# A graph network in two layers: one tile in four chunks of the second layer built by TensorE, its weight matmuls split in 64-row pairs, and the one-hots beside the early chunks made by ScalarE

## The reference

```
h  = max(layernorm(x), 0)
x += relu((segment_sum((h * norm_src)[src], dst) * norm_dst) @ weight + bias)        # layer 0
h  = max(layernorm(x), 0)
w  = (relu(edge_attr_32 @ W1 + b1) @ W2 + b2).reshape(e, 4, 8, 8)                    # per edge
m0 = ALPHA * (einsum(s[src] * sh0, w_000) + C110 * einsum(v[src], sh1, w_110))
m1 = ALPHA * (einsum(s[src], sh1, w_011) + einsum(v[src] * sh0, w_101))
x += segment_sum([m0, m1], dst) + SI_SCALE * (h through si_w0, si_w1)                # layer 1
```

## Time and profile before

| | |
|---|---|
| median of three runs | 4124.31 us |
| the profiled execution | 4122.98 us |
| its span (first to last instruction) | 4121.1 us |
| busy: PE, DVE, ACT, POOL | 3132.6, 2649.4, 1693.6, 3087.7 us |
| layer 0: early chunks gathered / beside early / alone | to 294 / 294 to 873 / 873 to 1978 us |
| layer 1: first to last gather | 1998.8 to 4092.6 us |
| granted TensorE clock, mean | 0.875 |

### The profile page before, as it was taken

One profiled execution on the slowest core, in us unless ns is written; L12 is line 12 of the kernel. 1 busy time (PEld: TensorE's weight loads), 2 busy tenths in 40 slices (PEclk: granted clock), 3 DMA queues, 4 the chain that ended last, 5 costly groups with the idle time before them and its releaser, 6 DMA issues.

```text
span 4121.1 us, 82454 instructions
## 1 busy us (share of the span) xinstructions
PE 3132.6 (76%) x20394; PEld 2298.3 (56%) x20395; DVE 2649.4 (64%) x5843; ACT 1693.6 (41%) x5935; POOL 3087.7 (75%) x3210
## 2 busy tenths in 40 slices
PE   5654444468777777777788888888888888888887
PEld 4544444444444443343466667666677667666676
DVE  8995444455555554454577777777777777777776
ACT  3210000013333333333655555555555555555554
POOL 7767777777777777777677777777777777777775
PEclk9996555568888888988899999999999999999999
DMA  2021111111111111111111111111111111111111
GB/s 56 14 54 39 38 38 38 38 27 23 22 23 23 22 23 22 21 22 21 26 30 28 28 28 29 30 28 28 29 30 29 28 28 29 30 28 28 29 30 18
DMA packets 244961, 119.57 MB, mean 29 GB/s; under 512 B 148880, under 2 KB 226065, under 8 KB 244817
## 3 DMA queue, kind: packets, MB, share of 16 engines
q0 software_dynamic: 102528, 52.70, 9.1%
q1 hardware_dynamic: 131625, 48.99, 5.1%
q10 hardware_dynamic: 10768, 17.44, 1.3%
HBM read 113.94 MB, written 4.92 MB: 29 GB/s over the span
## 4 chain that ended last, share of the span: by engine, by line
POOL 59%; issue 24%; DVE 8%; PE 3%; DMA 1%; DVEq 1%; ACT 1%; POOLq 1%; ACTq 0%; SPq 0%
POOL g L447 59%; DVE acc_b L952 4%; DMA g<-table,idx 1%; PE ps L704 1%; PE ps L738 1%; PE ps L772 1%; ACT onehot L579 1%; DVEq L952 0%; ACT onehot L586 0%; DVE hn L1212 0%; DVE prod_a L1066 0%; DVE ef L1195 0%; ACT root L557 0%; DVE stat L905 0%; DVE stat L902 0%
## 5 line engine op out<-in xcount | busy, mean ns | idle before, releaser
L447 POOL DMA_INDIRECT g<-table,idx x2980 | 2872.1, 964 | 935.1 <-issue 902.5
L828 PE MATMUL ps<-w_s,hid 128*128 128x256 f32 x3328 | 884.8, 417 | 270.0 <-ACT hid L627 220.8
L828 PEld LDWEIGHTS ps<-w_s,hid 128*128 128x128 f32 x3328 | 660.4, 207 | 437.5 <-DVE prod_a L1270 231.3
L579 ACT ACTIVATE onehot<-iota_all,dst_rel 128x68 f32<-128x68 f32 x2648 | 673.8, 337 | 384.4 <-DVEq L1132 319.8
L639 ACT ACTIVATE q<-g,sh 128x32 f32<-128x32 f32 x1664 | 375.4, 308 | 861.5 <-DMA g<-table,idx 861.5
L738 PE MATMUL ps<-split_s,prod_a 128*128 128x512 bf16 x1736 | 572.7, 415 | 34.4 <-DVE prod_a L1057 33.5
L1275 DVE TENSOR_REDUCE msg_b<-prod_b 128x128 f32<-128x1024 f32 x416 | 502.1, 1207 | 0.0
L704 PE MATMUL ps<-onehot,g 128*33 128x68 f32 x2880 | 269.4, 263 | 273.8 <-issue 173.8
L1245 DVE TENSOR_TENSOR vsh<-g,sh 128x192 f32<-128x192 f32 x208 | 81.7, 393 | 580.1 <-ACT q L642 580.1
L704 PEld LDWEIGHTS ps<-onehot,prod_a 128*128 128x128 f32 x3328 | 388.8, 192 | 86.1 <-issue 86.0
L704 PEld LDWEIGHTS ps<-onehot,g 128*33 128x33 f32 x2880 | 233.4, 137 | 344.1 <-issue 327.5
(11 more groups left out here) (132 smaller groups left out, 3437.3 us busy)
## 6 DMA issues: line engine op xcount, KB each, us to landing
g<-table,idx POOLq DMA_INDIRECT x2980
ef<-edge_t SPq DMA_DIRECT2D x208, 128.0 KB
ef<-src_rows ACTq DMA_DIRECT2D x27, 512.0 KB, 3.6
prod_a<-src_rows SPq DMA_DIRECT2D x124, 64.0 KB, 3.0
idx<-src_chunks SPq DMA_DIRECT2D x416, 4.0 KB
g<-x_rows,idx POOLq DMA_INDIRECT x224
sh<-sh_chunks SPq DMA_DIRECT2D x208, 16.0 KB
table<-hn ACTq DMA_DIRECT2D x5, 320.0 KB, 3.5
```

What stands on the lines that cost most here:

```text
L447: pool.indirect_dma_start(out=g[:, j, t, 0:FEAT], out_offset=None, in_=table, in_offset=bass.IndirectOffsetOnAxis(ap=idx[:, j, t:t + 1], a ...
L579: ins = act.activation(onehot[:, b, t, :], iota_all[:, 0:WIN], ACT.Square, scale=-1.0, bias=dst_rel[:, bass.ds(c * TILES + t, 1)])
L828: mm = pe.matmul(w_ps[h][:, t, :], hid[:, h, P * t:P * t + P], w2_s[:, :], start=True, stop=True)
```

## The change

1. In layer 1, from the third iteration on (`ROWS_FROM = 2`, so 50 iterations), the eighth tile of the fourth chunk (`ROWS_AT = 3`) is no longer gathered. It is built as in layer 0: VectorE splits table2 into three bfloat16 parts during the first seven chunks (`split_group`), makes the 7 selection matrices at the end of the fourth chunk (`make_source2`), TensorE runs the 21 matmuls behind the window sums of the first chunk (`source_rows2`), VectorE picks the rows at the end of the second (`choose2`). SyncE loads the groups of table2 and the source numbers, in its queue between the loads that were there.
2. The 256 weights: the hidden values of the two halves of a chunk now lie in partitions 0 to 63 and 64 to 127 of `hid`, `w2_s` stands there twice, and the eight matmuls are four pairs of 64 rows. The bias no longer fits in as a row, so four bfloat16 matmuls of 32 rows by 512 columns write it first, from a tile of ones and b2 in three parts; VectorE prepares that after layer 0. Both halves are asked for in one piece: TensorE waits until both relus are done and both halves of the weights before have been used. The two halves of the hidden layer go to different partitions of one PSUM bank, where they had a bank each; the other bank takes the built rows.
3. In `beside_early` the one-hots come from ScalarE, as in `alone`, and ScalarE's loads of early sources stand between them.
4. The last step of a block writes x in place of xc.

```diff
+    def rows_made_in(i):
+        return not isinstance(i, int) or i >= ROWS_FROM
...
-                    for t in range(tiles):
+                    for t in range(MADE if rows_made and j == ROWS_AT else tiles):
                         pool.indirect_dma_start(
...
+            def onehots_beside(i):
+                for pos in range(len(UNITS)):
...
+                    wait(act, joined1, n)
+                    distances(2 * i + nxt_k if nxt_early else RING * nxt_i + (EARLY + nxt_k),
+                              1 - pos % 2).then_inc(squares1_made, 1)
+                    act.wait_ge(squares1_made, n + 1)
+                    ones_at_zero(1 - pos % 2).then_inc(onehot1_ready, 1)
+                    if nxt_early and not (isinstance(i, int) and 2 * i + nxt_k == EARLY - 1):
+                        next_sources(2 * i + nxt_k)
...
-                        mm = pe.matmul(ps[0:HID, H_BANK + h, at:at + 256], w1_s[row:row + 32, :],
+                        mm = pe.matmul(ps[HID * h:HID * h + HID, H_BANK, at:at + 256], w1_s[row:row + 32, :],
                                        ef[row:row + 32, 512 * (j // 2) + at:512 * (j // 2) + at + 256], start=True,
-                                       stop=True, tile_position=(row, 0))
+                                       stop=True, tile_position=(row, HID * h))
...
-                k = 2 * (RING * i + j) + h
-                pe.wait_ge(hidden_ready, k + 1)
-                wait(pe, weights_used, k - 1)
+                k = 2 * (RING * i + j)
+                pe.wait_ge(hidden_ready, k + 2)
+                wait(pe, weights_used, k)
+                for u in range(4):
+                    h, t = u % 2, u // 2 * 2
+                    rows = slice(32 * u, 32 * u + 32)
+                    pe.matmul(w_ps[h][:, t:t + 2, :], ones_b[rows, :], bias_b[rows, :, :], start=True, stop=False,
+                              tile_position=(32 * u, 0), skip_group_check=True)
                 for t in range(4):
-                    mm = pe.matmul(w_ps[h][:, t, :], hid[:, h, P * t:P * t + P], w2_s[:, :], start=True, stop=True)
-                mm.then_inc(weights_ready, 1)
+                    for h in range(2):
+                        rows = slice(HID * h, HID * h + HID)
+                        mm = pe.matmul(w_ps[h][:, t, :], hid[rows, 0, P * t:P * t + P], w2_s[rows, :], start=False,
+                                       stop=True, tile_position=(HID * h, 0), skip_group_check=True)
...
+            def source_rows2(m):
+                pe.wait_ge(split2_done, GROUPS)
+                pe.wait_ge(source2_ready, m + 1)
+                for k in range(GROUPS):
+                    for n in range(3):
+                        mm = pe.matmul(rows2_ps, source2[:, k, :], split[n][:, k, :],
+                                       start=(k == 0 and n == 0), stop=(k == GROUPS - 1 and n == 2))
...
                     window_sums(c, messages_of(b), j, b, seg2_done, 1)
+                    if j == 0 and rows_made_in(i):
+                        source_rows2(i - ROWS_FROM)
...
+                    if isinstance(c, int) and c < GROUPS:
+                        split_group(c)
+                    if j == ROWS_AT - 2 and rows_made_in(i):
+                        choose2(i - ROWS_FROM, RING * i + ROWS_AT)
+                    if j == ROWS_AT and not (isinstance(i, int) and not ROWS_FROM - 1 <= i < ITERS - 1):
+                        make_source2(i - (ROWS_FROM - 1))
```

More of the change, by code:

```diff
@@ L262, in over_iterations, with over_layer2 @@
             body(ITERS - 1)
+        def over_layer2(eng, body):
+            for i in range(ROWS_FROM):
+                body(i)
+            with eng.Fori(ROWS_FROM, ITERS - 1) as i:
+                body(i)
+            body(ITERS - 1)
+        def rows_made_in(i):
+            return not isinstance(i, int) or i >= ROWS_FROM
         def final_blocks(eng, c):
@@ L437, in _, with gather @@
                       allow_small_or_imprecise_dtypes=True).then_inc(iota_done, 1)
-            def gather(i, table, iteration, free, tiles=TILES):
+            def gather(i, table, iteration, free, tiles=TILES, rows_made=False):
                 for j in range(RING):
@@ L483, in _ @@
             pool.wait_ge(table2_out, 16 * BLOCKS)
-            over_iterations(pool, lambda i: gather(
-                i, table2, i + ITERS, lambda c, j: wait(pool, d_ready, c - RING + 1)))
+            over_layer2(pool, lambda i: gather(
+                i, table2, i + ITERS, lambda c, j: wait(pool, d_ready, c - RING + 1),
+                rows_made=rows_made_in(i)))
         @block.scalar
@@ L838, in layer2 @@
                     b = j % 2
[L839 to L840 removed]
+                    weights(i + (j + 1) // RING, (j + 1) % RING)
                     hidden(i + (j + 2) // RING, (j + 2) % RING)
@@ L1235, in _ @@
             link(dve.tensor_scalar(w2_s[:, 64:256], w2_s[:, 64:256], float(ALPHA), None, ALU.mult))
+            dve.wait_ge(bias_in, 16)
+            link(dve.memset(ones_b, 1.0))
+            link(dve.tensor_scalar(bias_f[:, 0:64], bias_f[:, 0:64], float(ALPHA * C110), None, ALU.mult))
+            link(dve.tensor_scalar(bias_f[:, 64:256], bias_f[:, 64:256], float(ALPHA), None, ALU.mult))
+            for k in range(3):
+                link(dve.tensor_copy(bias_part, bias_f))
+                if k < 2:
+                    link(dve.tensor_tensor(bias_f, bias_f, bias_part, ALU.subtract))
+                for u in range(2):
+                    if k == 0:
+                        link(dve.tensor_scalar(bias_b[:, u, :], bias_part, masks[:, 0:1], None, ALU.mult))
+                    else:
+                        link(dve.scalar_tensor_tensor(out=bias_b[:, u, :], in0=bias_part, scalar=masks[:, k:k + 1],
+                                                      in1=bias_b[:, u, :], op0=ALU.mult, op1=ALU.add))
@@ L1236, in _, with split_group @@
             dve.tensor_scalar(sel_b_s[64:96, :], sel_b_s[64:96, :], float(SI_SCALE), None,
                               ALU.mult).then_inc(weights_scaled, 1)
+            def split_group(k):
+                n = group_rows(k)
+                full = stage2[k % 2][0:n, :]
+                high, middle, rest = (part_s[0:n, k, :] for part_s in split)
+                dve.wait_ge(whole2_in[k % 2], 16 * (k // 2 + 1))
+                link(dve.tensor_copy(high, full))
+                link(dve.tensor_tensor(full, full, high, ALU.subtract))
+                link(dve.tensor_copy(middle, full))
+                dve.tensor_tensor(rest, full, middle, ALU.subtract).then_inc(split2_done, 1)
@@ new lines, in make_source2 @@
+            def make_source2(m):
+                dve.wait_ge(keys2_in, 16 * (m + 1))
+                dve.tensor_scalar(key2, keys2, GROUP_LOG, None, ALU.logical_shift_right).then_inc(key2_ready, 1)
+                dve.wait_ge(key2_ready, m + 1)
+                for k in range(0, GROUPS, 2):
+                    n = min(2, GROUPS - k)
+                    ins = dve.tensor_tensor(source2[:, k:k + n, :], key2[:, None, :].to_broadcast([P, n, P]),
+                                            first[:, k:k + n, None].to_broadcast([P, n, P]), ALU.is_equal)
+                ins.then_inc(source2_ready, 1)
```

165 lines of the change are left out of this document (113 added, 52 removed).

## The result

The changed kernel takes 4222.4 us (median of 4, 4207.5 to 4236.4) where the kernel before took 4124.4: the ratio is 1.0236, with an interval of 1.021 to 1.0261. I had predicted 4057 us and given slower a chance of 0.13. The profiled execution took 4210.9 us, span 4209.1, which is 87.9 more than the profiled execution before.

A forecast was written before the change was run, and what follows sets the result against it. It took GpSimd's gather line, 59% of the chain of waits, as the bound: 4122.98 - 62.9 (gathers) - 12 (one-hots) + 5 (VectorE in layer 1) + 1 (rest) + 3 (even race) = 4057.1 us, range 4037 to 4122.

The forecast's parts named there:

- 50 x 1.259: GpSimd in layer 1: 50 iterations lose one gather of 1.259 us each, 62.9 us saved.
- the condition beside it: A removed gather pays only while TensorE, VectorE and ScalarE can use a chunk faster than GpSimd fetches it.
- part 2: Layer 1's consumers: whether they can follow GpSimd's shortened iteration of 39.0 us; 38.3 forecast, a cover of 0.7 us.
- x = 2.45: Length of TensorE's one-piece weights group per chunk with bias, paired matmuls overlapping: 2.45 us, between 2.2 and 4.6.
- the 38.3: Consumers' iteration in us: four rounds 30.0, built tile 3.6 late, selection matrices and choice 3.9, output 0.8.
- these steps keep their length: Behind the last gather: the 28 us there were to stay as they were.
- Rival A: VectorE's wait for weights: pairs don't overlap or bias is slow; slower, 4341 us at its point; chance 0.13.
- rival B: TensorE: x 2.6 to 3.0, hidden layer unpaired or lower clock; 4060 to 4125 us; chance 0.27.
- One-hots, -12: Early stretch: VectorE one-hots hold up gathers, so moving them to ScalarE saves 12 us.
- rival C: Early stretch: one-hots on VectorE cost gathers nothing, so 4069 us; chance 0.10.
- +5 for VectorE's work in layer 1: The 50 built tiles' VectorE work holds up gathers in layer 1, 0.10 us each: 5 us added.
- +1 for the rest: Splitting table2, preparing the bias and SyncE's new loads: 1 us added, from 0 to +6.

The follow-up runs named there:

- e2: The changed kernel with weights made as before the change, 128-row, unpaired, each half asked for by itself; built tiles stay: 4061.5 us, ratio 0.9847.
- h1: The changed kernel with ten unread matmuls ahead of TensorE's wait before the weights of chunks 1 and 3: 4107.2 us, ratio 0.996.
- e3: The changed kernel with pairs laid over two tiles of the same half, so each half is asked for alone: 4098.7 us, ratio 0.9949.
- h5: e3 with seven unread matmuls in chunk 1 ahead of the second half's weights: 4070.9 us, ratio 0.9865.
- h3: e2 with the joined wait of the changed kernel, its weights still unpaired: 4162.6 us, ratio 1.0076.
- h4: The kernel before with only the one-hots beside early chunks moved to ScalarE: 4121.5 us against 4132.6, ratio 0.9976.
- e1: The changed kernel without the built tile in layer 1, all eight tiles of every chunk gathered again: 4113.0 us, ratio 0.9974.
- e5: The changed kernel with ten unread matmuls ahead of TensorE's wait for VectorE in chunks 0 and 1: 4178.6 us, ratio 1.013.

## Why the prediction was wrong

By its own steps.

- **Gathers, 50 x 1.259.** The number was right and the condition beside it broke. Where the consumers can follow (e2) layer 1 from first to last gather takes 2039.2 us, where 2093.8 - 62.9 + 5 + 3 = 2038.9 was forecast.
- **The step that failed** is in part 2: "so I expect the 0.96 of full speed of the earlier trace rows to stay". It was 0.87 in layer 1, and 0.96 to 0.97 again in h1. I took the mean demand of TensorE, 82% by my count, for what its clock goes by. But the change turns TensorE's work into bursts with longer gaps between them, and it was in the groups behind the gaps that the clock fell. Before, TensorE's 3.72 us of weights came in two parts, the first of them while VectorE was still busy; afterwards one part of 2.4 us stands in a queue behind VectorE, and where VectorE has a selection matrix or a choice inserted, TensorE idles for 3.2 to 3.6 us and falls to the lower level. Together with the groups behind output blocks, two of four groups have x = 0.46 + 3.43 = 3.9 us.
- **x = 2.45** was right at the clock it was worked out for: 2.00 for the weights and 0.32 to 0.39 for the bias, 2.36 from the first bias matmul to VectorE's product in h1 (3007.34 to 3009.70). Pairs do run beside each other. Against the rule of the Trainium skill that I had weighed, that different row tiles can't use one PSUM bank at the same time (TensorEngine Tiling (Array Packing), Gotcha 1), the hidden layer's halves, which share a bank but not their partitions, take 1.08 us as before.
- **The rest of the 38.3.** Put the two slow rounds at full clock, 7.21 as in h1 for chunk 1 and 9.06 - 1.65 = 7.4 for chunk 3: 9.73 + 7.21 + 13.99 + 7.41 = 38.3. Its parts were off, though. Plain rounds are shorter (7.21, not 7.49) and the built tile and the choice dearer (13.99 - 7.21 = 6.8, where 3.6 and half of 3.9 were forecast); the agreement of the sum is partly luck.
- **What the slow groups cost.** 41.65 instead of 39.0 is 2.65 us an iteration, 132 over 50; the miss in layer 1 is 2167.9 - 2038.9 = 129. The other 25.5 stand behind the last gather. I had written that these steps keep their length, but when GpSimd isn't the last any more, it ends with its slots full, and several chunks are still to be worked off: VectorE had one chunk's last product before it when the last gather started before, and four now, 54.0 us. Even in e2, at even pace, two are left, and it is 34.7 us. The sum is 154.5, against 153.8 that the profiled execution is over the forecast.
- **Rival A named the place and the wrong reason.** It had VectorE's wait for the weights, the loss of the lead, and "from x = 3.05 on the kernel is slower". What it asked for was pairs that don't overlap. They overlap; it is the clock that makes x 3.9 in every second round, 3.1 in the mean, just beyond that point. A lower clock stood in rival B with a price of at most 1.5 us an iteration, and no working for why it would fall.
- **How much is clock and how much lead** can't be split in two amounts, since either, given back, recovers most of it: 124 us for the lead (e3), 115 for the clock (h1), 151.5 for both (h5), and the joined wait also costs with unpaired weights (h3). It is one loop with three links, lead, length of the group and clock, and it must be under 39.0 us. Of the 50 us that h1 stays over the forecast, 22 stand behind the last gather (50.8 us, four chunks); the other 27 are its 39.67 us an iteration. Presumably these are the fillers' own cost in chunk 3 and the lead; which share, no run tells. Nor was a kernel tried in which the choice and the selection matrices are taken off VectorE.
- **One-hots, -12.** Measured -13.0 in the early stretch of the changed kernel, -10 to -11 by themselves (h4) and with the pairs (e1). Matching each one-hot with the gather that starts under it, as in the earlier trace rows, gave 13.5. VectorE's even share (6.3) was too low, and rival C, the page's inference that such a tensor_tensor doesn't hold GpSimd's descriptors (the Trainium skill, SBUF — State Buffer, Who interferes with whom), isn't borne out: taking these instructions off VectorE is worth 10 us, and brings a gather of that stretch from 1.011 to 0.983 us. What it is that holds the gather, no run shows.
- **+5 for VectorE's work in layer 1, +1 for the rest.** Not seen apart from the rest; e2's layer 1 is within 0.3 us of the sum that has them, and its layer 0 alone takes 1095.2 us, 0.7 more than before.

## What to carry to other kernels

Where two engines wait for each other in turn, work out the clock for the longest gap of the one with the matmuls, from its place in the loop, and not from the share of busy time; price each group behind a long gap at both levels (here 2.00 and up to 3.79 us), and ask whether the sum still fits at the lower one. A faster group of matmuls gains nothing when it must wait for its consumer: the kernel with old, longer weights and their lead was the fastest of all. And an edit that takes work from the bound should be tried without the edit that is meant to make room for it; here the cover (39.0 against the consumers) was enough without it.

## What the runs showed of the hardware

- Groups of the same matmuls took 2.00 us or up to 3.79, by what TensorE did before. Behind up to 0.96 us of idling 96 of 100 ran at full speed throughout, behind more than 3 us none of 82 did (2.82 to 3.79 us). In the case shown from e3, behind 2.17 us of idling, the fall came 1.4 us after work had begun again.
- TensorE fell with hardly any idling, too: behind a block of output (3.9 us of matmuls of 32 columns, each behind a load of 128, with at most 0.22 us of idling ahead of them) all 24 groups of weights ran at the lower level in whole or in part, 3.10 to 3.79 us. An example of the changed kernel, the last two rows of such a block and the group behind it:

```profile
3065.00 0.63 PE L964 MATMUL ps<-sel_b_s,hn 96*128 96x32 f32 x2
3065.56 0.39 PE L912 MATMUL ps<-hid 32*128 32x512 bf16 x4
3065.89 3.37 PE L917 MATMUL ps<-w_s,hid 64*128 64x256 f32 x16
```

- Useless matmuls in a gap pay: 115 us in h1, 28 us from e3 to h5. Where TensorE had hardly idled they cost as much as they take (e5, chunk 0: +1.65 us).
- Two row groups of 64 with float32 took 2.00 us, 2.33 with the bias matmuls, for the work that took 3.72 as one group of 128 rows with the bias in it.
